# The edge features' product, split into end rows first and source rows later

## The chip, the cores and the metric

The kernel runs on one core of a Trainium2 chip. The metric is the device time of one execution in microseconds (us), lower is better. The times are the median of several runs; the profile is of one further execution, whose times are counted from the start of its span.

## The reference

A graph network and two more layers run on 625 nodes with 512 features. The part that matters here is the attention over 10,000 edges in the second block. Cut to it:

```
h_e = einsum('nf,hfd->hnd', x, W_e)          # 8 heads of 64
h_r = einsum('nf,hfd->hnd', x, W_r)
s_src = einsum('hnd,hd->hn', h_e, a_src)[:, src]
s_dst = einsum('hnd,hd->hn', h_e, a_dst)[:, dst]
diff = h_r[:, dst] - h_r[:, src]
score = s_src + s_dst + einsum('hed,hd->he', diff, a_dif) \
      + einsum('hed,hd->he', abs(diff), a_abs) \
      + einsum('hed,hd->he', h_r[:, src] * h_r[:, dst], a_prd)
alpha = leaky_relu(score, 0.2)
# softmax over the edges of one src, then the sum of att * h_e[dst] into src
```

Beside it stands a linear attention over all nodes (q, k, v from the same normalised x, softmax of k over the nodes, context, output product), whose result is added to x as well.

## The kernel before

The 625 nodes are five tiles of 125 partitions (`NT`), the 512 features four chunks of 128 (`KC`). Each engine has its own block of instructions, and semaphores tie them together. PSUM is a ring of four slots of two banks: `psum_jobs()` lists all uses of it in the order of TensorE's queue, each with the engine (`act` or `dve`) that empties it. `claim` lets TensorE wait until the job that had the slot before has been emptied. Jobs named in `BESIDE_EDGES` share two slots only, since the edge turns hold the other two.

Before the edges, the normalised x is transposed tile by tile (`xnT`, 2). Then TensorE makes `hre`: for each tile a product with `wer`, 1024 columns, the source rows W_e in columns 0 to 511 and the end rows W_r in 512 to 1023. ScalarE copies the W_r half into `hrx` (L1280) and rounds it into `hr_high` (L1283); GpSimd makes the rest `hr_low` (L668). SyncE stores `hrx` to `table` in DRAM. VectorE copies the W_e half into `hea` (L1793), forms per tile three products with the vectors in `ar` (L1799), a difference (L1805) and two reductions (L1802, L1807). The results are the linear terms of the score, one for the node as source and one as destination, in the columns `HD` and `HD + 1` of `hrx`. VectorE then prepares casts and constants and signals `tmp_free` (L1825), since `tmp` lies where the gathers land.

The edges are then taken in 40 turns of 250 edges (`TURNS`), half of them by gathers and half by products:

- GpSimd gathers rows of `table` for both ends (L680), four turns ahead, and scatters the scores into `pairs` (L690), each scatter after the landing of the one before it of the same kind.
- VectorE makes one-hots of the other 125 edges (L1863, L1866). TensorE transposes them (`edge_turn`, L960), ScalarE copies them (L1291), and TensorE multiplies them with `hr_high` and `hr_low` (`edge_product`, L973). VectorE then weighs and reduces both halves (L1872, L1896, L1880).
- Into TensorE's queue, at fixed turns, are put the products of the linear attention: `KEYS`, `QUERIES` (L757), `VALUES` (L748, emptied by VectorE at L1835), `KEYS_TURNED` (L740), `CONTEXT` (L998, emptied at L1846), `ATTENDED`, `PROJECTED` and the transposes `ROWS_TURNED`, which read `hrx` with its linear terms.

TensorE makes the transpose of turn e + 1 before the product of turn e. After the last turn the scattered pairs are loaded and merged (L1930), and a stage over pairs of nodes follows, in which `hea` is multiplied with the weights (L1068).

Of the kernel before, what the change touches and what calls it, by code (L numbers as in the profile page):

```python
# [35 lines left out]
P = 125  # L36
# [54 lines left out]
BESIDE_EDGES = ("kT", "qT", "v1", "kn", "ctx", "oT", "y1", "rT")  # L91

KEYS = (1, 3, 5, 7)
# [11 lines left out]
def psum_jobs():  # L105
# [19 lines left out]
    jobs += [(("hre", i), "dve") for i in range(NT)]  # L125
    for e in range(PROJECTED[-1] + 1):
        for turns, name, who in ((KEYS, "kT", "act"), (QUERIES, "qT", "act"),
# [95 lines left out]
def build_gps(nc, a, out):  # L223
    with ExitStack() as ctx:
# [147 lines left out]
        ar = view(9096, 4, D, parts=P)  # L372
# [3 lines left out]
        tmp = view(18944, 3, D, parts=P)  # L376
# [3 lines left out]
        edge_hots = [view(4220 + N * n, N, parts=P).bitcast(F16)  # L380
# [83 lines left out]
        def _(sp):  # L464
# [68 lines left out]
            for n, name in enumerate(("a_abs", "a_src", "a_dst", "a_dif")):  # L533
                load(ar[:, n, :], row(name), "gat_loaded")
# [4 lines left out]
            for i in range(NT):  # L539
# [3 lines left out]
                load(t[112:P], hrx[112:P, i, :, 0:HD], "table_stored")  # L543
            load(wo1, w("w_outT"), "wo1_loaded")
# [45 lines left out]
        def _(pool):  # L590
# [75 lines left out]
            for i in range(NT):  # L666
                pool.wait_ge(sig("hr_high_ready"), i + 1)
# [28 lines left out]
            pool.wait_ge(sig("tmp_free"), 1)  # L696
# [33 lines left out]
        def _(pe):  # L730
# [217 lines left out]
            for i in range(NT):  # L948
                slot = ring.claim(pe, ("hre", i))
                ring.wait_emptied(pe, ("xnT", 2, i))  # L950
                ring.filled(product(slot, P, nodes(xnT, i), lambda k: wer[:, k, :], KC, 2 * D))
# [13 lines left out]
            def edge_product(e):  # L965
# [10 lines left out]
                last.then_inc(sig("edge_product"), 1)  # L976

# [37 lines left out]
            ring.wait_emptied(pe, ("hre", NT - 1))  # L1015
            pe.wait_ge(sig("hrx_ready"), NT)
            edge_turn(0)
            pe.wait_ge(sig("hr_low_ready"), NT)
            pe.wait_ge(sig("mix1_loaded"), 32)
            for e in range(PROJECTED[-1] + 1):  # L1020
                if e + 1 < TURNS:
                    edge_turn(e + 1)
                if e < TURNS:
                    edge_product(e)
                if e in KEYS:
                    key_or_query("kT", D, KEYS.index(e))
# [10 lines left out]
                if e in ROWS_TURNED:  # L1037
                    h = ROWS_TURNED.index(e)
                    turn(("rT", h), lambda k: hrx[:, k, h, :], [HX] * NT, lambda k: 128 * k)
# [62 lines left out]
        def _(act):  # L1102
# [175 lines left out]
            for i in range(NT):  # L1278
                slot = ring.wait_filled(act, ("hre", i))
                act.activation(hrx[:, i, :, 0:HD],  # L1280
                               slot[0:P, D:2 * D].rearrange("p (h e) -> p h e", h=H), ACT.Copy)\
                   .then_inc(sig("hr_copied"), 1)
                act.activation(hr_high[:, i, :], slot[0:P, D:2 * D], ACT.Copy)\  # L1283
                   .then_inc(sig("hr_high_ready"), 1)
# [794 lines left out]
```

## Time and profile before

| what | us |
|---|---|
| median of 3 runs | 1088.94 |
| lowest and highest | 1088.46, 1090.07 |
| profiled execution, its own time | 1090.06 |
| its span | 1088.2 |
| TensorE matmuls busy (90%) | 982.1 |
| VectorE busy (70%) | 764.0 |
| GpSimd busy (32%) | 347.5 |
| ScalarE busy (31%) | 336.0 |

Shares are of the span. A busy share says how full an engine is on average over stages of different kinds, and not what sets the end. The profile's chain of waits gives TensorE 43%, VectorE 27%, GpSimd 14% and DMA 7% of the span. TensorE's mean granted clock is 0.959 of full speed (2.4 GHz). In a row, the number in square brackets is the idle time of the engine before this instruction and what ended it; an fp32 matmul has two records.

### The profile page before, as it was taken

The numbers are of one execution on the slowest core, as the hardware profiler recorded it, in microseconds if no ns is written. First come the engines' busy times: TensorE is split into PE (matmuls) and PEld (weight loads), VectorE is DVE, ScalarE is ACT, GpSimd is POOL, SyncE is SP. The second block draws the span as 40 slices with busy tenths as digits, with TensorE's granted clock in tenths as the row PEclk, the third lists the DMA queues.
The fourth block names the chain that finished last, engine by engine and source line by source line (L and its number), as shares of the span: only waits on it lengthen the run. The fifth ranks groups of instructions, "written<-read, shape, count | busy, mean of one in ns | idle before, by whom it ended". The sixth has DMA issues, their size and how long they took to land.

```text
span 1088.2 us, 12200 instructions
## 1 busy us (share of the span) xinstructions
PE 982.1 (90%) x4284; PEld 648.8 (60%) x4284; DVE 764.0 (70%) x1320; ACT 336.0 (31%) x613; POOL 347.5 (32%) x316
## 2 busy tenths in 40 slices
PE   7899999999899989999896988999887859988988
PEld 6874686544574447544463436776565528877864
DVE  8897697333795667744435468998987759999743
ACT  5873472312402231122114111321113303444511
POOL 1007720000301102001100116777777714555500
PEclk9999999999999999999898998999988976999999
DMA  9999210203300222001130325333333377541101
GB/s 306 294 306 274 64 79 1 85 12 115 126 1 1 91 59 90 1 0 56 48 115 1 134 48 155 99 99 98 98 93 95 89 284 292 207 163 40 63 1 47
DMA packets 66036, 115.10 MB, mean 106 GB/s; under 512 B 11473, under 2 KB 43473, under 8 KB 64445
## 3 DMA queue, kind: packets, MB, share of 16 engines
q1 hardware_dynamic: 57021, 93.08, 25.3%
q0 software_dynamic: 8960, 21.31, 7.1%
q8 instruction: 32, 0.52, 0.2%
q14 instruction: 23, 0.19, 0.1%
HBM read 85.88 MB, written 28.49 MB: 105 GB/s over the span
## 4 chain that ended last, share of the span: by engine, by line
PE 43%; DVE 27%; POOL 14%; issue 8%; DMA 7%; ACT 1%; SPq 0%; POOLq 0%; DVEq 0%; ACTq 0%
PE ps L748 17%; PE ps L886 7%; POOL arena L680 7%; DMA pairs<-arena,pairi 5%; PE ps L757 5%; DVE arena L1589 5%; POOL pairs L690 4%; PE ps L791 3%; PE ps L740 3%; DVE arena L1945 3%; DVE arena L1930 2%; PE ps L940 2%; DVE arena L1954 2%; PE ps L1093 2%; POOL small L639 1%
## 5 line engine op out<-in xcount | busy, mean ns | idle before, releaser
L748 PE MATMUL ps<-arena 128*125 128x512 f32 x400 | 179.7, 605 | 0.8 <-DVE xn L1623 0.8
L616 POOL TENSOR_TENSOR small<-small 125x1 f32<-125x1 f32 x50 | 34.9, 698 | 390.4 <-DVE small L1402 390.4
L748 PE MATMUL ps<-arena,xnT 128*125 128x512 f32 x280 | 125.7, 607 | 5.0 <-DVE x L1856 4.2
L748 PEld LDWEIGHTS ps<-arena 128*125 128x125 f32 x400 | 75.5, 193 | 90.2 <-issue 89.2
L973 PE MATMUL ps<-ex_low,high 125*125 125x512 f32 x400 | 107.3, 416 | 0.0
L1248 ACT ACTIVATE arena<-ps,cols 128x125 f32<-128x125 f32 x120 | 43.2, 466 | 202.9 <-PE ps L740 202.9
L748 PEld LDWEIGHTS ps<-arena,xnT 128*125 128x125 f32 x280 | 53.5, 193 | 70.4 <-issue 69.0
L690 POOL DMA_INDIRECT pairs<-arena,pairi x80 | 86.9, 1086 | 25.5 <-issue 25.5
L740 PE MATMUL ps<-ident,arena 125*125 125x125 f32 (+3 forms) x425 | 63.0, 285 | 26.5 <-ACT arena L1105 8.8
L973 PEld LDWEIGHTS ps<-ex_low,high 125*125 125x125 f32 x400 | 74.6, 195 | 16.7 <-issue 0.5
L740 PEld LDWEIGHTS ps<-ident,arena 125*125 125x125 f32 (+3 forms) x425 | 54.4, 170 | 48.8 <-issue 17.3
L1105 ACT ACTIVATE arena<-ps 125x625 f32<-125x625 f32 (+4 forms) x79 | 49.3, 648 | 108.1 <-PE ps L740 90.6
L715 POOL TENSOR_TENSOR arena<-arena,counts 125x625 f32<-125x625 f32 x40 | 57.4, 1436 | 78.6 <-ACT arena L1356 35.5
L757 PE MATMUL ps<-arena 66*125 66x313 f32 (+3 forms) x176 | 61.0, 475 | 17.3 <-DVE small L1945 8.6
L886 PE MATMUL ps<-arena 128*125 128x512 f32 x160 | 70.5, 593 | 1.7 <-DVE arena L1594 1.7
L791 PE MATMUL ps<-arena 125*125 125x314 f16 x400 | 57.3, 305 | 6.8 <-DVE arena L1445 5.7
L791 PEld LDWEIGHTS ps<-arena 125*125 125x125 f16 x400 | 54.9, 140 | 9.1 <-DVE arena L1445 7.1
L1356 ACT ACTIVATE arena<-arena,small 125x625 f32<-125x625 f32 x40 | 32.7, 818 | 86.7 <-DVE arena L1954 86.7
L1657 DVE TENSOR_TENSOR x<-x,ps 125x512 f32<-125x512 f32 x30 | 20.5, 685 | 55.1 <-PE ps L748 23.3
L1681 DVE TENSOR_TENSOR arena<-ps,arena 125x512 f32<-125x512 f32 x15 | 10.4, 691 | 65.0 <-PE ps L748 65.0
L1880 DVE TENSOR_REDUCE arena<-arena 125x8 f32<-125x512 f32 x80 | 54.6, 682 | 1.4
L1945 DVE CUSTOM_DVE_ANT_0 arena<-ps,arena 125x625 f32<-125x625 f32 x40 | 51.6, 1290 | 2.3 <-PE ps L757 2.1
(215 smaller groups left out, 1811.6 us busy)
## 6 DMA issues: line engine op xcount, KB each, us to landing
pairs<-fill SPq DMA_DIRECT2D x10, 2500.0 KB, 21.9
arena<-in_mw SPq DMA_DIRECT2D x6, 2048.0 KB, 8.4
arena<-pairs SPq DMA_DIRECT2D x4, 2500.0 KB, 13.9
arena<-pairs SPq DMA_DIRECT2D x8, 1250.0 KB, 6.0
arena<-pairs SPq DMA_DIRECT2D x8, 625.0 KB, 6.4
arena<-in_rows SPq DMA_DIRECT2D x16, 250.0 KB
arena<-in_qkv_w SPq DMA_DIRECT2D x1, 3072.0 KB
arena<-in_cw SPq DMA_DIRECT2D x3, 1024.0 KB, 5.3
```

Source lines behind the costliest of these rows:

```text
L680: pool.indirect_dma_start(out=rows[:, g % GATHERS, :], out_offset=None, in_=table, in_offset=bass.IndirectOffsetOnAxis(ap=ends[:, 2 * g:2 ...
L690: pool.indirect_dma_start(out=pairs[n], out_offset=bass.IndirectOffsetOnAxis(ap=pairi[:, t:t + 1], axis=0), in_=sc[:, t % SCORES, :], in_o ...
L715: pool.tensor_tensor(Sg, Sg, counts[:, i, 0:N].bitcast(F32), ALU.mult).then_inc(sig("pair_weighted"), 1)
L740: last = pe.transpose(slot[0:n, at:at + rows], src, ident[0:rows, 0:rows])
L748: last = mm(slot[0:m, lo:hi], lhsT_of(k), rhs_of(k)[:, lo:hi], start=(k == 0), stop=(k == ks - 1))
L757: last = mm(slot[0:m, at + lo:at + hi], lhsT_of(k), rhs_of(k)[:, lo:hi], start=(k == 0), stop=(k == ks - 1))
L791: last = mm(ps[0:P, 512 * i:512 * i + HALF], one_hot[:, k, 0, P * i:P * (i + 1)], one_hot[:, k, 1, 0:HALF], start=False, stop=False, skip_ ...
L886: last = mm(slot[0:P, lo:lo + 512], nodes(hT, i)(k), w1[:, k, lo:lo + 512], start=(k == 0), stop=(k == KC - 1))
L973: last = mm(product_at[0:P, at:at + D], hotsT[e % 2][:, i, :], part[:, i, :], start=(part is hr_high and i == 0), stop=(part is hr_low and ...
L1589: st.did(v.reciprocal(r, r))
L1880: v.tensor_reduce(sc[0:P, t % SCORES, :], src.rearrange("p (h e) -> p h e", h=H), AX_X, ALU.add)\
L1945: ring.emptied(v.tensor_tensor_reduce(Sg, slot[0:P, across_banks(N)], p3[:, :, h], -1.0, 3e38, ALU.add, ALU.min, smax[:, 0, h:h + 1]), ("p ...
```

## The change

The product `hre` is split. First come the end rows alone, one product of 512 columns per tile (`hr`), emptied by ScalarE. The source rows are a job of their own (`he`, function `sources`), for tile 0 before the first turn's product and for the other tiles in turns 0, 25, 27 and 28 (`HE`). They share the two slots of the linear attention and are emptied by ScalarE, which writes `hea`.

The linear terms are no longer formed from the rows. Since they are linear in the normalised x, the vectors are multiplied into the weights instead: VectorE folds `wer` with `a_dst` (`fold_destinations`, between the normalisations of the tiles) and with `a_src` and `a_dif` minus `a_abs` (`fold_sources`, after the first one-hots) into 16 columns per chunk, `terms`. `sources` multiplies these along with the source rows, and ScalarE copies the 16 results into `hrx`. The vectors are loaded over 128 partitions. `tmp` and its signal `tmp_free` are gone. The edge one-hots move to another place in SBUF; the load of `w_outT` now waits until the last source rows are there, since it overwrites `wer`.

```
-    jobs += [(("hre", i), "dve") for i in range(NT)]
+HE = (-1, 0, 25, 27, 28)
+    jobs += [(("hr", i), "act") for i in range(NT)] + [(("he", 0), "act")]
...
@@ SyncE
+            ring.wait_emptied(sp, ("he", NT - 1))
             load(wo1, w("w_outT"), "wo1_loaded")
...
@@ GpSimd
-            pool.wait_ge(sig("tmp_free"), 1)
             pool.wait_ge(sig("spare_loaded"), 32)
...
@@ TensorE
-                ring.filled(product(slot, P, nodes(xnT, i), lambda k: wer[:, k, :], KC, 2 * D))
+                ring.filled(product(slot, P, nodes(xnT, i), lambda k: wer[:, k, D:2 * D], KC, D))
...
+            def sources(i):
+                slot = ring.claim(pe, ("he", i))
+                for k in range(KC):
+                    mm(slot[0:P, 0:D], xnT[:, k, P * i:P * (i + 1)], wer[:, k, 0:D],
+                       start=(k == 0), stop=(k == KC - 1))
+                    last = mm(slot[0:P, D:D + 2 * H], xnT[:, k, P * i:P * (i + 1)],
+                              terms[:, k].rearrange("p n h -> p (n h)"),
+                              start=(k == 0), stop=(k == KC - 1))
+                ring.filled(last)
...
-            ring.wait_emptied(pe, ("hre", NT - 1))
-            pe.wait_ge(sig("hrx_ready"), NT)
+            ring.wait_emptied(pe, ("hr", NT - 1))
             edge_turn(0)
+            pe.wait_ge(sig("terms_ready"), KC)
+            sources(0)
             pe.wait_ge(sig("hr_low_ready"), NT)
             pe.wait_ge(sig("mix1_loaded"), 32)
             for e in range(PROJECTED[-1] + 1):
                 if e + 1 < TURNS:
                     edge_turn(e + 1)
                 if e < TURNS:
                     edge_product(e)
+                if e in HE:
+                    sources(HE.index(e))
...
@@ ScalarE
+            def sources(i):
+                if i == 0:
+                    act.wait_ge(sig("hea_ready"), 2)
+                slot = ring.wait_filled(act, ("he", i))
+                act.activation(hea4[:, i, :, 0:HD],
+                               slot[0:P, 0:D].rearrange("p (h e) -> p h e", h=H), ACT.Copy)
+                ring.emptied(act.activation(
+                    hrx[:, i, :, HD:HX],
+                    slot[0:P, D:D + 2 * H].rearrange("p (n h) -> p h n", n=2), ACT.Copy), ("he", i))
...
@@ VectorE
+            def fold_destinations(k):
+                st.did(TT(folds[:, 0, :], wer[:, k, 0:D], a_ends[:, 1, :], ALU.mult))
+                st.wait()
+                v.tensor_reduce(terms[:, k, 0, :], by_head(folds[:, 0, :]), AX_X, ALU.add)\
+                    .then_inc(sig("folded"), 1)
+                v.wait_ge(sig("folded"), k + 1)
+            def fold_sources(k):
+                st.did(TT(folds[:, 1, :], wer[:, k, 0:D], a_ends[:, 0, :], ALU.mult))
+                st.did(TT(folds[:, 2, :], wer[:, k, D:2 * D], a_ends[:, 2, :], ALU.mult))
+                st.wait()
+                st.did(TT(folds[:, 1, :], folds[:, 1, :], folds[:, 2, :], ALU.subtract))
+                st.wait()
+                v.tensor_reduce(terms[:, k, 1, :], by_head(folds[:, 1, :]), AX_X, ALU.add)\
+                    .then_inc(sig("terms_ready"), 1)
+                v.wait_ge(sig("terms_ready"), k + 1)
             for i in range(NT):
                 add_to_x(("f0o", i), i)
                 ring.wait_emptied(v, ("f0o", i))
                 stats_of_x(i)
                 if i:
                     normed_x(i - 1)
+                    fold_destinations(i - 1)
             normed_x(NT - 1)
-            for i in range(NT):
-                slot = ring.wait_filled(v, ("hre", i))
-                v.wait_ge(sig("hr_high_ready"), i + 1)
-                ring.emptied(v.tensor_copy(hea4[:, i, :, 0:HD],
...
...
             one_hots_of_edges(0)
             one_hots_of_edges(1)
+            for k in range(KC):
+                fold_sources(k)
```

## Rows read from the trace of the kernel before

**Rows 1.** Chain of waits, from 596 us: start, us, what.
```profile
613.37 34.96 PE ps L748 x80
...
655.93 0.03 DVEq L1825
...
656.94 1.57 POOL arena L680
```
**Rows 2.** Windows of the edge turns: busy us of each engine, clock, DMA.
```profile
700.00:750.00 50.00, 49.36 (x236) 36.66 (x235) 44.62 (x72) 12.70 (x20) 39.03 (x37) 1.00 0.35 97
750.00:800.00 50.00, 44.56 (x198) 30.41 (x197) 45.07 (x74) 9.25 (x14) 38.72 (x38) 0.95 0.36 99
```
**Rows 3.** Timeline, ScalarE's copy of tile 2, TensorE's first turns: start, us, instruction.
```profile
634.62 0.60 ACT L1280 ACTIVATE arena<-ps 125x512 f32<-125x512 f32 x1 [5.78 <-PE ps L748]
...
657.49 0.76 PE L960 MATMUL ps<-arena 125*125 125x125 f16 x5 [9.18 <-DVE arena L1866]
...
659.65 3.75 PE L973 MATMUL ps<-ex_low,high 125*125 125x512 f32 x10
```
**Rows 4.** Window of half a us after tile 2's store; last column GB/s.
```profile
638.50:639.00 0.50, 0.50 (x2) 0.19 (x1) 0.47 (x2) 0.00 (x0) 0.00 (x0) 1.00 0.01 2
```
**Rows 5.** Timeline, VectorE's last two normalisations before the edges.
```profile
610.36 0.54 DVE L1410 TENSOR_SCALAR xn<-x,small 125x512 f32<-125x512 f32 x1
...
611.34 0.88 DVE L1410 TENSOR_SCALAR xn<-x,small 125x512 f32<-125x512 f32 x1 [0.44 <-POOL small L616]
```
**Rows 6.** Narrow matmuls in the chain; VectorE's groups: busy, mean ns.
```profile
189.73 1.72 PE ps L838 x16
...
907.67 2.05 PE ps L1068 x10
...
L1799 DVE TENSOR_TENSOR arena<-arena 125x512 f32<-125x512 f32 x15 | 10.8, 769 | 0.2
...
L1880 DVE TENSOR_REDUCE arena<-arena 125x8 f32<-125x512 f32 x80 | 54.6, 682 | 1.4
```
**Rows 7.** Timeline of GpSimd, scatters of turns 2, 31 and 39.
```profile
678.67 0.99 POOL L690 DMA_INDIRECT pairs<-arena,pairi  x1 [0.31 <-issue]
...
838.64 0.99 POOL L690 DMA_INDIRECT pairs<-arena,pairi  x1 [0.30 <-issue]
...
875.69 0.97 POOL L690 DMA_INDIRECT pairs<-arena,pairi  x1 [0.34 <-issue]
```
**Rows 8.** Timeline of VectorE in the edge turns; last, the merges' group.
```profile
675.61 0.69 DVE L1880 TENSOR_REDUCE arena<-arena 125x8 f32<-125x512 f32 x1
...
783.82 0.69 DVE L1896 TENSOR_TENSOR arena<-arena 125x512 f32<-125x512 f32 x1 [0.94 <-DMA arena<-table,dsti]
...
817.34 0.69 DVE L1896 TENSOR_TENSOR arena<-arena 125x512 f32<-125x512 f32 x1 [0.88 <-DMA arena<-table,dsti]
...
828.58 0.69 DVE L1872 SCALAR_TENSOR_TENSOR arena<-ps,arena 125x512 f32<-125x512 f32 x1 [4.25 <-PE ps L973]
...
870.15 0.69 DVE L1872 SCALAR_TENSOR_TENSOR arena<-ps,arena 125x512 f32<-125x512 f32 x1 [3.48 <-PE ps L973]
...
L1930 DVE TENSOR_TENSOR arena<-arena 125x625 f32<-125x625 f32 x40 | 34.6, 880 | 2.7 <-DMA arena<-pairs 2.7
```
**Rows 9.** Timeline of TensorE in the edge turns.
```profile
706.25 4.37 PE L757 MATMUL ps<-xnT,arena 128*128 128x312 f32 x16
710.47 0.45 PE L960 MATMUL ps<-arena 125*125 125x125 f16 x5
...
715.81 4.37 PE L757 MATMUL ps<-xnT,arena 128*128 128x312 f32 x16
...
787.17 0.78 PE L740 MATMUL ps<-ident,arena 128*125 128x128 f32 x5 [1.97 <-DVE xn L1835]
...
788.97 3.94 PE L973 MATMUL ps<-ex_low,high 125*125 125x512 f32 x10
...
822.99 2.45 PE L757 MATMUL ps<-arena 128*128 128x312 f32 x4 [8.18 <-DVE arena L1846]
```

More of the change, by code:

```diff
@@ L124, in psum_jobs @@
                    lambda i: [], lambda i: [(("xnT", 2, i), "act")])
-    jobs += [(("hre", i), "dve") for i in range(NT)]
+    jobs += [(("hr", i), "act") for i in range(NT)] + [(("he", 0), "act")]
     for e in range(PROJECTED[-1] + 1):
-        for turns, name, who in ((KEYS, "kT", "act"), (QUERIES, "qT", "act"),
+        for turns, name, who in ((HE, "he", "act"), (KEYS, "kT", "act"), (QUERIES, "qT", "act"),
                                  (VALUES, "v1", "dve"), (KEYS_TURNED, "kn", "act"),
@@ L371, in build_gps @@
         wer = view(5000, KC, 2 * D)
-        ar = view(9096, 4, D, parts=P)
+        a_abs = view(9096, D)
+        a_ends = view(24100, 3, D)
+        folds = view(0, 3, D)
+        terms = small[:, 128:192].rearrange("p (k n h) -> p k n h", k=KC, n=2)
         hea = view(11144, NT * H * (HD + 1) + WIDE - HD - 1, parts=P)
@@ L532, in _ @@
             load(wer, w("w_er"), "gat_loaded")
-            for n, name in enumerate(("a_abs", "a_src", "a_dst", "a_dif")):
-                load(ar[:, n, :], row(name), "gat_loaded")
+            load(a_abs, row("a_abs", 128), "gat_loaded")
+            for n, name in enumerate(("a_src", "a_dst", "a_dif")):
+                load(a_ends[:, n, :], row(name, 128), "gat_loaded")
             ring.wait_emptied(sp, ("f0o", NT - 1))
@@ L948, in _ @@
             for i in range(NT):
-                slot = ring.claim(pe, ("hre", i))
+                slot = ring.claim(pe, ("hr", i))
                 ring.wait_emptied(pe, ("xnT", 2, i))
-                ring.filled(product(slot, P, nodes(xnT, i), lambda k: wer[:, k, :], KC, 2 * D))
+                ring.filled(product(slot, P, nodes(xnT, i), lambda k: wer[:, k, D:2 * D], KC, D))
             turned, product_at = ring.psum[2], ring.psum[3]
@@ L1329, in _ @@
                     edge_turned(e)
+                if e - 1 in HE:
+                    sources(HE.index(e - 1))
                 if e - 1 in KEYS:
@@ L1822, in _ @@
             st.did(v.memset(sc, 0.0))
+            flat = hea[:, 0:NT * H * (HD + 1)]
+            v.memset(flat.rearrange("p (g e) -> p g e", e=HD + 1)[:, :, HD:HD + 1], 1.0)\
+                .then_inc(sig("hea_ready"), 1)
+            v.memset(hea[:, NT * H * (HD + 1):], 0.0).then_inc(sig("hea_ready"), 1)
+            st.did(TT(a_ends[:, 2, :], a_ends[:, 2, :], a_abs, ALU.subtract))
+            st.did(TS(a_abs, a_abs, 2.0, None, ALU.mult))
             st.did(TS(minus_ident, ident[0:P, 0:P], -1.0, None, ALU.mult))
             st.wait()
-            v.sem_inc(sig("tmp_free"), 1)
             def k_largest(j):
```

47 lines of the change are left out of this document (12 added, 35 removed).

## The prediction, on record before the result

> **What bounds the kernel now.** I read the chain of waits first, for the stretch from the end of the first expert layer to the edge turns. One piece stands out, TensorE's 80 matmul records of the `hre` products, 34.96 us; then VectorE's work on the last tile; then the queue of VectorE, whose `tmp_free` lets GpSimd begin its gathers at 656.94 [rows 1]. From there the chain runs through GpSimd's gathers and scatters and their landings for all 40 turns. A product of 512 columns costs 0.43 us per record: 34.96 / 80 = 0.437, of which 0.65 us is a start at the lower clock.
>
> Second, who is how far ahead in the edge turns. GpSimd starts the scatter of turn 2 at 678.67, of turn 31 at 838.64 and of turn 39 at 875.69, so (838.64 - 678.67) / 29 = 5.5 us per turn while it also gathers [rows 7]. VectorE has turn 2's score at 675.61 + 0.69 = 676.30, 2.4 us before GpSimd starts on it; turn 31's at 828.58 + 3.2 = 831.8 (from the read of PSUM to the last reduction are five instructions of 0.68 to 0.69 us each, slightly overlapping, 3.2 us), 6.8 us early; turn 39's at 870.15 + 3.2 = 873.35, only 2.3 us early [rows 7, 8]. So GpSimd sets the pace, but at both ends of the loop another engine is close behind. That engine is TensorE: it is busy 49.36 of 50 us around turns 8 to 17 and 44.56 in the next 50 [rows 2]. There, a key or query product takes 710.47 - 706.25 = 4.22 us, and two times `edge_turn` with its product 715.81 - 710.47 = 5.34, 2.67 each [rows 9]. From turn 22 to 30 it has slack: VectorE waits for gathers [rows 8], and TensorE waits 1.97 us before turn 26 and 8.18 us for the context [rows 9]. From turn 31 to 39 it is dense again, so what TensorE is late at turn 31 it is late at turn 39.
>
> **Part by part.** (All times in the profiled execution of before: span 1088.2, run 1090.06 us.)
>
> *First tile data.* `fold_destinations` puts a product and a reduction, 0.69 to 0.77 and 0.69 us [rows 6], into each of four passes of VectorE. Three lie where VectorE waits for `f0o`. The fourth lies between the two normalisations at 610.36 and 611.34, where VectorE had 0.4 us of room [rows 5]: tile 4's comes about 1.0 us later, and TensorE's transpose, on the path, with it. Nothing else queued there.
>
> *End rows.* Five products of 512 columns instead of 1024 remove 40 records of 0.43: -17.2 us. The last product ends at 648.33 + 1.0 - 17.1 = 632.2; a longer stay at the low clock may add up to 1 us, I take 0.2. ScalarE's two copies now release the slots: `hr_copied` at 633.0.
>
> *GpSimd's start.* `tmp_free` is gone; what is late next is `table_stored`. In before, tile 2's copy ends at 634.62 + 0.60 = 635.2 [rows 3] and the traffic of its store has ended by 638.5 [rows 4], some 3.4 us. So the table is stored at 636.4 and, with the 0.98 us from VectorE's signal to the first gather [rows 1], the gathers begin at 637.5: 19.4 us earlier. The loads of w_qkvT come before in the same queue and have ended by then. The load of w_outT now waits for the last `sources` (turn 28) and is wanted at turn 34, some 27 us later: nothing.
>
> *VectorE's preparation.* Removed are five tiles of copy, four products or sums and two reductions. Added are `fold_sources`, four times three products and a reduction, about 2.8 us each, 11.2 in all, behind some 2.6 us of casts and memsets and two pairs of one-hots (2.4 us): from 613.2 to about 629.5. TensorE asks for the terms at 633.9, so 4 us cover it; the first sources would wait for what exceeds that.
>
> The folds run beside GpSimd's subtractions, as L1799 did, which took 0.77 us in the mean [rows 6]; three of those per chunk instead of 0.69 are 1 us in all, within the cover. The Trainium skill (GPSIMD Engine Reference, its table at the top) says that GpSimd's SBUF interface is shared with VectorE and contended by instructions with two SBUF inputs, which these are; the row agrees.
>
> *Sources.* Each is four products of 512 columns (3.44 us) and four of 16. No row has 16 columns. The nearest are 96 wide: 16 records (8 matmuls) in 1.72 us, 0.215 us each, and 10 records in 2.05 us, 0.41 each, both from the chain [rows 6]. From below, 16/512 of a wide one would be 0.03. I take 0.215, the 96-wide matmul at its fastest, which a narrower one should not exceed. So a `sources` is 4.3 us (3.6 to 5.1), five are 21.5: more than was removed. The Trainium skill (TensorE: Matmul & The Clock Gate, LDWEIGHTS) says that loading weights scales with their columns, however few columns are streamed; with 125 columns at its rate, twice per fp32 matmul, its estimate is 0.21 us. By the columns streamed alone a `sources` would be 3.6 us; by that page it is the 4.3 that I take.
>
> *The first turns.* TensorE: `edge_turn(0)` from 633.5 (last slot emptied) to 633.95, sources(0) to 638.3, then turn 1 and product 0 to 641.0, sources(1) to 645.3, product 1 to 647.9, key 0 to 652.1. In before product 0 began at 659.65 and took 3.6 us to the next instruction [rows 3]; with 2.67 and 4.22 key 0 ended at 670.1. So TensorE's path is 18.0 us earlier against 19.4 for GpSimd. That includes two gains: in before TensorE idled 9.18 us and ran the first product at the low clock, 3.75 us [rows 3]. Turn 2's margin falls from 2.4 to 1.0 us, it still holds, and grows from there as before.
>
> *The late sources* (in before's times less 19.4, so that GpSimd's own column is unchanged). TensorE's lag of 1.4 is used up by turn 24, where VectorE waited 0.94 us for its gather [rows 8], and less than that a turn earlier. sources(2) starts when v1's slot is free, 787.2, and ends 791.5; kn(1) and product 26 end at 794.9; kn(2), product 27 at 798.2; sources(3), kn(3), product 28 at 805.8; sources(4) at 810.1, product 29 at 812.8, the context at 817.3, product 30 at 820.0. In before VectorE had turn 30's gather, the last that it waited for, at 817.34 [rows 8]; now it gets there at 820.0 + 0.6 = 820.6, 3.3 us later. So 12.9 us of products cost 3.3: the waits of rows 9, and the gather waits, take the rest. The first may run low: product 26 took 3.94 us after the wait of 1.97 [rows 9], and sources(2) may meet that clock, up to 2.5 us more. I take 0.8: TensorE is 4.1 us late at turn 31, whose margin of 6.8 holds.
>
> *The end of the loop.* 4.1 late at turn 39 against a margin of 2.3, with 0.2 us of hand-over: 2.0 us lost. VectorE's last sums into x are then 2.1 us behind the loads of the pairs; VectorE waits 2.7 us for these loads at the first merges [rows 8], so that is hidden. The pair stage and all behind it don't change.
>
> **Sum.** -19.4 + 2.0 = -17.4; 1090.06 - 17.4 = 1072.7. The profiled run is 1.1 above the median of 1088.94, so 1071.5 us.
>
> **Rivals.** (A) TensorE's path becomes the bound sooner: `sources` is 5.1 us and the low clock meets sources(2). Then the first two cost 1.6 us more, the three late ones 2.4, the low clock 1.7: TensorE is up to 4.1 + 5.7 = 9.8 us late at turn 39, 7.7 lost, a gain of 11.7: 1077. For it speaks the 2.05 us row; against it that the 1.72 us row shows 16 narrow records in a row at half that price.
> (B) The work is only moved: none of the late sources falls into a wait, 12.9 + 1.4 = 14.3 us late at turn 39, 12.2 lost, a gain of 7: 1082. Against it stand the 8.18 us, though these are a wait for VectorE's context, which moves along.
> (C) No change: the first gathers still wait, for a term or store that lands near 656. The folds would have to end some 22 us later, or the stores 19 us: 1089. I see nothing for it.
> (D) Slower: TensorE holds 1.2 GHz over all five `sources`, 8.6 us each (twice 4.3), 21.5 us more. Added to the 4.1, and less what turns 22 to 30 absorb (none is left), it is 25.6 late, less 2.3: 23 lost against 19.4, +4: 1093. It decides from 19.4 + 2.1 = 21.5 us late at turn 39. A fall to the low clock is seen after idle only, and the products fill idle: little for it.
>
> **How the numbers follow.** My forecast 0.64, with its own range 1068.5 to 1074.5 (weight price down to 3.6, first start 1 us earlier or later); A 0.22; B 0.08; C 0.03; D 0.03. The range is 1068.5 to 1078, it leaves out B to D and the tails. A measurement can tell 0.2%, 2.2 us, from no change: faster 0.94, same 0.03, slower 0.03.
>
> **What would show it.** Right: one `hr` block of 17 to 18 us ending near 632; the first gather near 637.5, led by a landing of table and not by VectorE; TensorE's gap before the first edge turn of 1 to 2 us; blocks of sources of 4.3 us; GpSimd's scatter of turn 38 some 19 us earlier, and before the last one a wait for VectorE. Wrong: a gap of TensorE before sources(0) (folds late), a first gather after 640 (stores), matmuls of 16 columns at 0.4 us, or scatters that wait for scores before turn 35.

## The result, and the profile after

The changed kernel takes 1073.25 us in the median of 4 runs (1071.32 to 1078.3), against 1088.7 for the kernel before (4 runs, 1087.45 to 1090.07): a ratio of 0.9865 with a 95% interval of 0.9829 to 0.9901, 1.35% faster. The profiled run took 1073.43 us, its span is 1071.6, and TensorE's mean granted clock 0.967. Against the profiled run of before that is 16.6 us less; the forecast from there was 17.4 less. A second set of 5 runs of the changed kernel (below) gave 1073.97; over both sets the median is 1073.8.

The chain of waits of the changed kernel, between the expert layer and the first gathers (start, us, what), answers to [rows 1]:

```profile
609.20 0.71 DVE stat L1429
...
611.39 0.69 DVE small L1812
...
612.71 1.09 PE ps L744 x4
613.80 19.16 PE ps L752 x40
...
634.23 2.65 DMA table<-arena
637.18 1.30 POOL arena L685
```

The 80 records of 34.96 us have become 40 of 19.16. VectorE's reductions and its signal are gone from the chain; the landing of the table stands in their place. The second line is the new fold of the fourth weight chunk: it lies on the path. 40 records at 0.43 would be 17.2 us; the other 2 us are the clock, as the windows show (after the stretch and its length: busy us of PE, PEld, DVE, ACT and POOL, then clock, DMA share, GB/s):

```profile
608.00:611.00 3.00, 0.99 (x6) 0.55 (x5) 2.42 (x6) 0.59 (x1) 0.62 (x1) 0.97 0.25 35
611.00:614.00 3.00, 2.19 (x9) 1.74 (x9) 2.87 (x14) 0.75 (x2) 0.79 (x2) 0.50 0.98 393
614.00:618.00 4.00, 4.00 (x6) 1.51 (x5) 3.90 (x8) 0.43 (x1) 0.00 (x0) 0.54 1.01 421
618.00:622.00 4.00, 4.00 (x10) 1.69 (x9) 3.90 (x6) 1.09 (x2) 1.52 (x1) 1.00 0.46 144
```

The third number from the right is the granted clock: 0.50 (1.2 GHz) from 611 until near 618, though TensorE is busy without a gap from 614 on.

TensorE at the start of the turns, in its timeline (in brackets the idle time before, and what ended it), and the group rows of the new matmuls:

```profile
634.12 0.50 PE L964 MATMUL ps<-arena 125*125 125x125 f16 x5 [1.18 <-ACT ex_low L1301]
634.46 1.07 PE L985 MATMUL ps<-arena,xnT 128*125 128x512 f32 x2
635.37 0.29 PE L987 MATMUL ps<-small,xnT 128*125 128x16 f32 x2
635.50 1.10 PE L985 MATMUL ps<-arena,xnT 128*125 128x512 f32 x2
...
638.74 0.48 PE L964 MATMUL ps<-arena 125*125 125x125 f16 x5
639.02 2.56 PE L977 MATMUL ps<-ex_low,high 125*125 125x512 f32 x10
```

```profile
L987 PEld LDWEIGHTS ps<-small,xnT 128*125 128x125 f32 x40 | 7.5, 187 | 9.7 <-issue 9.7
...
L987 PE MATMUL ps<-small,xnT 128*125 128x16 f32 x40 | 5.8, 219 | 0.0
```

One `sources` is 638.74 - 634.46 = 4.28 us. From wide matmul to wide matmul it is 1.08 us at most places, so the narrow one adds 1.08 - 0.86 = 0.22 us. No wait for a term stands before it, and the first product takes 2.56 us where before it took 3.75 [rows 3].

Later, VectorE's copy of the values, VectorE's context and GpSimd's scatters (three timelines: TensorE's, the queue of SP, and GpSimd's):

```profile
767.98 1.12 PE L985 MATMUL ps<-arena,xnT 128*125 128x512 f32 x2 [1.05 <-DVE xn L1865]
...
806.88 2.45 PE L761 MATMUL ps<-arena 128*128 128x312 f32 x4 [6.35 <-DVE arena L1876]
...
809.62 3.74 PE L977 MATMUL ps<-ex_low,high 125*125 125x512 f32 x10
```

```profile
791.43 0.39 SPq L469 DMA_DIRECT2D arena<-in_w_outT  x1
```

```profile
796.67 1.48 POOL L695 DMA_INDIRECT pairs<-arena,pairi  x1 [0.76 <-DMA pairs<-arena,pairi]
799.78 0.99 POOL L695 DMA_INDIRECT pairs<-arena,pairi  x1 [1.63 <-DMA pairs<-arena,pairi]
```

The waits of 1.97 and 8.18 us [rows 9] have become 1.05 and 6.35: the late source rows filled part of them. The two scatters wait for the landing of the scatter before, a wait that the kernel before has nowhere near this place. They come just behind the load of w_outT. The window of these 4 us shows the traffic that they meet (columns as above):

```profile
794.00:798.00 4.00, 4.00 (x41) 4.00 (x39) 2.77 (x6) 0.00 (x0) 2.93 (x3) 1.00 1.01 308
```

It has 308 GB/s and all DMA engines full, where the same 4 us of the clock before move 43 GB/s.

The last turn, in the timelines of VectorE and GpSimd, and VectorE's merges:

```profile
855.16 0.69 DVE L1902 SCALAR_TENSOR_TENSOR arena<-ps,arena 125x512 f32<-125x512 f32 x1 [3.57 <-PE ps L977]
...
857.68 0.69 DVE L1910 TENSOR_REDUCE arena<-arena 125x8 f32<-125x512 f32 x1
...
877.92 1.53 DVE L1962 TENSOR_TENSOR arena<-arena 125x625 f32<-125x625 f32 x2 [3.01 <-DMA arena<-pairs]
```

```profile
859.29 0.97 POOL L695 DMA_INDIRECT pairs<-arena,pairi  x1 [0.51 <-issue]
```

Turn 39's score is ready at 857.68 + 0.69 = 858.37 and its scatter starts at 859.29, 0.92 us later; before, 2.34 lay between them [rows 7, 8].

Where the 16.6 us of the two profiles come from: first gather 656.94 to 637.18, -19.76; scatter of turn 39 counted from the first gather, 218.75 to 222.11, +3.36; from there to the pair stage +0.87; from the pair stage to the end of the span 193.18 to 192.11, -1.07. Sum -16.6.

### The profile page after: what moved, and what is told of

Its sections match the earlier page's. It is cut to its first block, busy times and chain, and to the rows that moved or that the text cites. A ratio compares the mean times of both kernels' runs of the same rounds, so it can differ in the third digit from the quotient of the medians.

```text
span 1071.6 us, 12287 instructions
## 1 busy us (share of the span) xinstructions
PE 979.7 (91%) x4324; PEld 648.0 (60%) x4324; DVE 759.3 (71%) x1309; ACT 338.8 (32%) x623; POOL 349.8 (33%) x316
## 4 chain that ended last, share of the span: by engine, by line
PE 40%; DVE 28%; POOL 14%; issue 8%; DMA 7%; ACT 1%; SPq 0%; POOLq 0%; DVEq 0%; ACTq 0%
PE ps L752 16%; PE ps L890 7%; POOL arena L685 6%; DMA pairs<-arena,pairi 5%; DVE arena L1620 5%; POOL pairs L695 4%; DVE arena L1977 4%; PE ps L761 4%; PE ps L795 3%; PE ps L744 3%; DVE arena L1962 2%; DVE arena L1986 2%; PE ps L944 2%; PE ps L1111 2%; POOL small L644 1%
## 5 line engine op out<-in xcount | busy, mean ns | idle before, releaser
L752 PEld LDWEIGHTS ps<-arena 128*125 128x125 f32 x400 | 75.6, 194 | 91.0 <-issue 89.8
L752 PE MATMUL ps<-arena,xnT 128*125 128x512 f32 x240 | 108.7, 610 | 5.0 <-DVE x L1886 4.2
L977 PE MATMUL ps<-ex_low,high 125*125 125x512 f32 x400 | 104.2, 406 | 0.0
L744 PE MATMUL ps<-ident,arena 125*125 125x125 f32 (+3 forms) x425 | 62.4, 283 | 25.9 <-ACT arena L1123 10.0
L752 PEld LDWEIGHTS ps<-arena,xnT 128*125 128x125 f32 x240 | 46.0, 194 | 60.9 <-issue 59.5
L744 PEld LDWEIGHTS ps<-ident,arena 125*125 125x125 f32 (+3 forms) x425 | 53.5, 168 | 47.7 <-issue 19.4
L977 PEld LDWEIGHTS ps<-ex_low,high 125*125 125x125 f32 x400 | 72.1, 188 | 15.9 <-issue 0.5
L761 PE MATMUL ps<-arena 66*125 66x313 f32 (+3 forms) x176 | 59.8, 468 | 16.2 <-DVE small L1977 8.2
L890 PEld LDWEIGHTS ps<-arena 128*125 128x125 f32 x160 | 29.6, 187 | 38.9 <-issue 35.8
```

Of the source, the lines that this page charges most:

```text
L744: last = pe.transpose(slot[0:n, at:at + rows], src, ident[0:rows, 0:rows])
L752: last = mm(slot[0:m, lo:hi], lhsT_of(k), rhs_of(k)[:, lo:hi], start=(k == 0), stop=(k == ks - 1))
L761: last = mm(slot[0:m, at + lo:at + hi], lhsT_of(k), rhs_of(k)[:, lo:hi], start=(k == 0), stop=(k == ks - 1))
L890: last = mm(slot[0:P, lo:lo + 512], nodes(hT, i)(k), w1[:, k, lo:lo + 512], start=(k == 0), stop=(k == KC - 1))
L977: last = mm(product_at[0:P, at:at + D], hotsT[e % 2][:, i, :], part[:, i, :], start=(part is hr_high and i == 0), stop=(part is hr_low and ...
```

## Experiments

All kernels were timed beside the kernel before, in three sets: after_again to both with 5 rounds (before: 1089.08), wout_twice to release_alone with 4 (1089.39), the last four with 4 (1089.56). One kernel's runs lie 2 to 10 us apart, so the stages inside the profiles are compared as well. A profile's span also holds differences that no edit explains: the fourth normalisation, up to which VectorE's program is the same in all kernels of the split, starts between 608.8 and 612.8 us. In the table, "norm to gather" runs from VectorE's fourth normalisation to GpSimd's first gather. The three columns after it are counted from the first gather: GpSimd's scatter of turn 31 (the first of the two scatters of the turn), turn 39's score ready, scatter of turn 39. "Falls" means that the granted clock goes to 0.50 there.

| kernel | median (low to high) | norm to gather | clock at 611 | scatter 31 | score 39 | scatter 39 |
|---|---|---|---|---|---|---|
| before | 1089.1 | 46.6 | falls | 181.7 | 216.4 | 218.8 |
| changed (first profile) | 1073.25 (1071.3 to 1078.3) | 26.96 | falls | 184.5 | 221.2 | 222.1 |
| after_again | 1073.97 (1072.1 to 1078.2) | 27.07 | falls | 183.2 | 221.3 | 221.6 |
| wout_mostly_early | 1069.92 (1068.2 to 1070.4) | 24.54 | stays | 184.0 | 220.8 | 221.7 |
| late_quarter | 1071.90 (1068.5 to 1076.0) | 26.97 | falls | 184.6 | 221.2 | 222.1 |
| both | 1071.42 (1068.2 to 1076.1) | 24.53 | stays | 183.3 | 218.1 | 220.4 |
| wout_twice | 1074.13 (1068.9 to 1074.7) | 24.55 | stays | 185.9 | 224.0 | 224.3 |
| all_first | 1083.62 (1079.4 to 1089.5) | 24.56 | stays | 196.5 | 231.3 | 233.5 |
| one_more_late | 1078.09 (1076.4 to 1080.9) | 27.01 | falls | 183.7 | 225.1 | 225.4 |
| release_alone | 1087.56 (1084.9 to 1093.3) | 41.24 | stays | 185.8 | 220.5 | 222.8 |
| fold_after | 1072.44 (1067.5 to 1073.0) | 25.00 | falls | 183.9 | 220.6 | 221.5 |
| wout_early_again | 1075.18 (1071.1 to 1075.3) | 27.00 | falls | 183.9 | 221.9 | 222.2 |
| best | 1069.90 (1067.6 to 1071.0) | 24.99 | falls | 182.6 | 220.6 | 220.8 |
| best_proj | 1072.10 (1069.7 to 1072.6) | 25.03 | falls | 184.7 | 220.5 | 223.1 |

**1. The changed kernel again** (after_again, no edit).

> The changed kernel once more, beside the others of this call. Each theory expects what its first runs gave: 1071 to 1075 us against about 1088.7 of before, the first gather near 637.2, the last scatter near 860.7 of the span.

The result repeats, ratio 0.9865 (0.9838 to 0.9892). It also gives the scatter between two profiles of one kernel: 1.3 us at the scatter of turn 31, 0.5 at that of turn 39.

**2. The load of w_outT placed early, the late source rows cut, and both.** The first edit:

```
+            for k in range(3):
+                load(wo1[k], w("w_outT")[:, k, :], "wo1_early")
...
-            load(wo1, w("w_outT"), "wo1_loaded")
+            load(wo1[3], w("w_outT")[:, 3, :], "wo1_loaded")
```

> Three of the four chunks of w_outT are loaded before the edge turns into other places, one chunk and b_out stay behind the last sources: 0.5 MB there instead of 1.25. Theory 1: the load beside turns 26 to 28 makes the scatters land late (waits of 0.76 and 1.63 us where 0.3 is usual), so GpSimd's scatter of turn 31 comes 1 to 1.5 us earlier against its first gather; but VectorE has turn 39's score only 0.9 us before GpSimd starts on it, so no more than 0.9 us reach the end: 0.3 to 0.9 us faster than the changed kernel. Rival: GpSimd was slower for another reason (its descriptor work beside more of VectorE's or TensorE's): scatter 31 stays where it is, same time.

The second edit leaves out three of the four chunks of the source rows' products of tiles 2 to 4:

```
-                for k in range(KC):
+                for k in range(KC if i < 2 else 1):
...
```

> The products of source rows for tiles 2 to 4 take one of four chunks only (the results of these tiles are wrong): 3.2 us less TensorE work in each of turns 25, 27 and 28, 9.7 in all. Theory 1: GpSimd's own chain sets the end of the turns by 0.9 us, so TensorE's work there is worth nothing: within 1 us of the changed kernel, though VectorE has turn 39's score some 3 to 5 us before GpSimd wants it. Rival (TensorE's path is the bound at turn 39, as the prediction had it): 2 us faster.

> Both edits: w_outT mostly loaded early, and a quarter of the late sources (results of tiles 2 to 4 wrong). Theory 1: with TensorE out of the way the whole of the load's price comes back, 1.5 to 2.5 us faster than the changed kernel, more than the two edits alone give in sum (0.3 to 0.9 and 0). Rival (one cause alone): the sum of the two.

The medians are 1069.92 (ratio 0.982, 0.9799 to 0.9842), 1071.9 (0.9843, 0.9812 to 0.9873) and 1071.42 (0.9848, 0.9823 to 0.9874): by them the three can hardly be told apart, and the stages must. In its first profile the early load took the waits for landings away between 775 and 830 us: no scatter there waits for one. Yet turn 39's score came at 220.8 after the first gather instead of 221.2. Cutting 9.7 us of TensorE's late work moved it not at all (221.2): there TensorE waits 2.56 us at 784 and 9.21 us for the context instead,

```profile
784.52 0.50 PE L964 MATMUL ps<-arena 125*125 125x125 f16 x5 [2.56 <-DVE arena L1897]
...
793.34 0.50 PE L964 MATMUL ps<-arena 125*125 125x125 f16 x5 [1.49 <-DVE arena L1897]
...
805.44 2.45 PE L761 MATMUL ps<-arena 128*128 128x312 f32 x4 [9.21 <-DVE arena L1877]
```

and one scatter still waits 2.29 us for a landing. (Above is TensorE's timeline in the kernel late_quarter.) Only both edits together bring 3.1 us, 218.1. So two things seem to lie side by side between turns 25 and 31, and whoever takes away one finds the other. That rests on one profile of each kernel; the score of turn 39 differs by only 0.1 us between the two profiles of the changed kernel. The first kernel's median was 4 us under the changed kernel's, which its score column cannot explain; 2.4 of the 4 lie in the stage before the first gather, where its edit does nothing that I can name. That led to experiment 7.

**3. The load made twice** (wout_twice: one more load of w_outT behind the first).

> The load of w_outT behind the last source rows is made twice, so that the traffic that meets the pairs' scatters lasts twice as long. If this load is what makes the scatters land late (theory), GpSimd's scatters near turns 27 to 30 wait 1.5 to 3 us longer for landings than in the changed kernel, and turn 31's scatter starts at 186.5 to 187.5 us after the first gather instead of 183.2 to 184.5; the end of the run moves by at most that, 0 to +2.5 us (1074 to 1076.5). If TensorE's late rows alone set the loop's end (rival), nothing moves by over 0.5 us. The clock of TensorE should fall at about 611 us as in the three kernels whose load stays in one piece behind the last source rows; if it does not, the placement of the load is not what decided that.

Missed in size: turn 31's scatter was expected at 186.5 to 187.5 and came at 185.9. Two scatters wait for landings, 1.34 and 1.65 us; in the changed kernel it is 0.76 and 1.63. From the second scatter of turn 24 to that of turn 31 it takes 41.0 us, as in the changed kernel (40.8 and 39.5 in its two profiles). Over the profiles of the split that stretch is 40.7 us in the mean with the late load (six profiles, 39.5 to 41.4) and 39.5 with three quarters of it early (five, 38.9 to 40.2); before it was 38.8. So the load costs GpSimd some 1.1 us, with ranges that overlap, and a second one adds nothing that shows. The clock at 611 us did not fall here, though the load is late: by the expectation's own test, the placement of the load does not decide that. What made this kernel's score 39 late by 2.8 us stands for the most part in TensorE's timeline: sources(2) came after a wait of 1.95 us instead of 1.05 and ran at the low clock at first, 6.0 us instead of 4.3.

```profile
766.52 1.35 PE L987 MATMUL ps<-arena,xnT 128*125 128x512 f32 x2 [1.95 <-DVE xn L1867]
767.66 0.44 PE L989 MATMUL ps<-small,xnT 128*125 128x16 f32 x2
767.95 2.05 PE L987 MATMUL ps<-arena,xnT 128*125 128x512 f32 x2
```

The Trainium skill (DMA: Bandwidth & Descriptors, SWDGE vs HWDGE vs iDMA) says that inside each DMA engine hardware and software queues feed different internal queues, between which the engine goes round robin. By that rule a scatter beside a load should get its turns, late but not stalled until the load has ended. The trace agrees in part. The changed kernel's traffic fills the DMA engines from 794 to 799. The scatter that starts at 790.85 has landed before 796.67, in the midst of it; the one that starts at 792.34 has landed only at 799.01, 6.67 us later (the median is 2.4), as the traffic ends. The second does not tell taking turns from waiting for the end.

**4. All source rows first** (all_first: the five products between the first transpose and the first product).

```
-HE = (-1, 0, 25, 27, 28)
+HE = ()
...
-            sources(0)
+            for i in range(NT):
+                sources(i)
```

> All five products of source rows stand between the first edge turn's transpose and its product, none later. If the four later ones cost TensorE little because they fall into waits there (theory, a price of about 4 us for 12.9 us of products), all of it now comes before the first product: product 0 starts about 17 us later than in the changed kernel, GpSimd's first score scatter too, and since GpSimd has four turns of gathers to do meanwhile, about 10 us of it show: 1082 to 1085. Rival: the place does not matter, because the same products are made and the loop has only to absorb them: 1074, within 2 us of the changed kernel.

As the theory had it: 1083.62, 9.8 us over the changed kernel's 1073.8. (Its runs lie 10 us apart, 1079.4 to 1089.5. Counted from the first gather, turn 39's scatter is 11.4 us later; in its profile the clock stayed up before the gathers, 2.4 us the other way. Its load of w_outT starts at 654.93, and so meets no late scatter.) The price stands in one line of GpSimd's timeline:

```profile
660.43 1.01 POOL L695 DMA_INDIRECT pairs<-arena,pairi  x1 [15.24 <-DVE arena L1912]
```

GpSimd has made its gathers ahead and waits 15 us for the first score. From the first scatter to turn 39's this kernel takes 208.2 us, as before (208.1); the changed kernel takes 210.8. So spreading takes away 14 us at the front and gives back 2.6 behind: placing products into waits is worth about 11.4 us here.

**5. One more source tile late** (one_more_late: tile 1 in turn 24 instead of turn 0, `HE = (-1, 24, 25, 27, 28)`).

> The source rows of tile 1 move from turn 0 to turn 24, nothing else. Theory (turns 22 to 30 of TensorE have room, the first turns have little): turn 2's scatter is no longer close behind its score, its margin goes from 0.7 to about 5 us; at the loop's end TensorE is 0 to 3 us later since its room is used up, so the time is 0 to +3 us against the changed kernel: 1074 to 1077. Rival (the room is not used up by three late ones): margins at turn 39 as in the changed kernel, 0.3 to 0.9 us, and no change within 1 us.

Even beyond the theory's upper end: 1078.09, 4.3 us more, one whole `sources`. Turn 2's margin went from 0.7 to 4.9 us, as expected, and was of no use. Turn 39's score is 3.9 us later. GpSimd shows it (its timeline, turn 39):

```profile
863.14 1.17 POOL L695 DMA_INDIRECT pairs<-arena,pairi  x1 [4.56 <-DVE arena L1910]
```

TensorE's timeline shows what the fourth late tile does, here and then in the changed kernel:

```profile
768.10 1.10 PE L744 MATMUL ps<-ident,arena 128*125 128x128 f32 x5 [2.29 <-DVE xn L1865]
...
772.96 1.02 PE L985 MATMUL ps<-arena,xnT 128*125 128x512 f32 x2
```

```profile
763.55 0.71 PE L744 MATMUL ps<-ident,arena 128*125 128x128 f32 x5
...
767.98 1.12 PE L985 MATMUL ps<-arena,xnT 128*125 128x512 f32 x2 [1.05 <-DVE xn L1865]
```

The source rows and the linear attention share two slots, so one more job in front shifts which job has to wait for VectorE's last copy of the values (L1865). In the changed kernel it is sources(2); here it is the turned keys (L744) one place earlier, and an edge turn with its product comes behind the wait too. These take 4.86 us from 768.10 to 772.96, against 3.2 for the same three at full speed, since the clock is low (0.53 of full speed from 769 to 772). Counted from the first gather, sources(2) starts 4.4 us later, of which 1.65 is the clock. So the fourth tile costs about its full length, by the shared slots and the clock; that the room itself is used up is not shown.

**6. The release alone** (release_alone: the kernel before, scratch moved away from the gathers' landing place, GpSimd's wait for it gone, products as before).

```
-        tmp = view(18944, 3, D, parts=P)
+        tmp = view(24100, 3, D, parts=P)
...
-            pool.wait_ge(sig("tmp_free"), 1)
...
-            v.sem_inc(sig("tmp_free"), 1)
```

> The kernel before with the two places of scratch moved apart, so that GpSimd's first gather no longer waits for VectorE's signal; products, linear terms and all else stay. The gather then waits for the last store of the table: about 3.6 us earlier, 653.3 instead of 656.9. Theory (before, GpSimd's column is 2.4 us behind TensorE's at turn 2 and at turn 39, so TensorE takes over when GpSimd starts earlier): 2.1 us of the 3.6 arrive, 1087.0 against 1089.1. Rival (GpSimd's start alone decides): all 3.6 arrive, 1085.5. Rival (the release was no part of the gain): 0.

Counted from the fourth normalisation, the first gather is 5.3 us earlier. From the end of the products it takes 650.57 - 646.24 = 4.3 us, against 656.94 - 648.33 = 8.6 before: 4.3 us are the release (I had put 3.6), and the other 1.0 goes with TensorE's clock, which stayed up. Then it is given back; the chain of waits of this kernel shows to whom:

```profile
611.89 34.35 PE ps L747 x80
...
657.93 3.92 PE ps L972 x10
...
665.37 1.01 POOL pairs L690
```

TensorE's products, through VectorE's term work, release the first scatter (it waits 4.16 us for the score), which comes 1.2 us earlier than before, counted from the same normalisation. The median is 1.8 us lower, ratio 0.9994 (0.9975 to 1.0013): no difference that these runs can tell. The 2.1 us of the theory and none at all both fit, the rival's 3.6 does not. In the kernel before, GpSimd's chain was only a few us longer than TensorE's; the release without the shorter products brings next to nothing. The other half, the split with the signal kept, was not run.

**7. The fold behind the last normalisation, and the load again.**

```
                 if i:
                     normed_x(i - 1)
+                if 0 < i < NT - 1:
                     fold_destinations(i - 1)
             normed_x(NT - 1)
+            fold_destinations(KC - 1)
```

> The changed kernel with the fold of the last chunk for the destinations put behind VectorE's last normalisation instead of before it. Theory (that fold delays the fifth tile's normalisation and with it the end rows' product by about 1 us, as predicted): the last normalisation starts about 0.8 us after the fourth one instead of 2.3, TensorE's last transpose and the product of the end rows about 0.9 to 1.3 us earlier, the first gather too; the run 0.9 us less, 1073.1 against 1074.0. Rival (the gap is set by GpSimd's statistics or by the slot that ScalarE empties, not by the fold): no change. Whether TensorE's clock falls at 611 us is a separate matter of about 2.4 us either way; it fell in four and did not fall in four of the eight profiles of kernels with the split so far.

> The kernel with three of the four chunks of w_outT loaded before the turns, a second time, on another run of the chip. If its 1069.9 was due to the placement of the load (theory A), it comes out at 1069 to 1071 again, 3 to 4 us under the changed kernel. If it was the clock at 611 us, which did not fall in that profile and did in the changed kernel's, and which the load cannot reach (theory B), the profile may show either, and the median lies between 1070 and 1074: the profile with a fall has its first gather 2.4 us later than the one without.

The gap between the last two normalisations went back from 1.89 to 0.98 us, as in before. From the fourth one to the first gather the kernel with the edit takes 25.0 us, with the clock falling, where the changed kernel takes 27.0 with the clock falling: 2.0 us for one product and one reduction of 1.4 us in sum. Against the profiles in which the clock stays (24.55, below) it is no gain, and no profile with the edit shows the clock staying. TensorE and the windows of the kernel best, which has the same edit, show how (columns as above; to be read against those of the changed kernel):

```profile
610.49 1.10 PE L746 MATMUL ps<-ident,xn 125*128 125x125 f32 x4 [2.01 <-DVE xn L1444]
611.82 1.09 PE L746 MATMUL ps<-ident,xn 125*128 125x125 f32 x4 [0.23 <-DVE xn L1444]
```

```profile
611.00:614.00 3.00, 2.77 (x9) 1.75 (x8) 2.87 (x8) 1.18 (x2) 0.48 (x1) 0.51 1.00 406
614.00:618.00 4.00, 4.00 (x10) 1.68 (x9) 3.89 (x14) 1.05 (x2) 0.00 (x0) 1.00 1.02 425
```

The fall itself is the same, but TensorE's second wait is 0.23 us instead of 0.81, and the clock is back at 614 instead of near 618. Of the 2.0 us, 0.6 is the later data (the normalised tile is there 1.86 instead of 2.44 us after the fourth normalisation began), the rest the shorter stay.

The repeated early load came out at 1075.18, not at 1069 to 1071, and its profile shows the fall and 27.0 us. So theory A is out. Theory B's sign is there, though the median is 1.2 us over its range. The same stretch in the first profile and then in the second (each time a line of TensorE's timeline and a window):

```profile
610.45 0.65 PE L746 MATMUL ps<-ident,xn 125*128 125x125 f32 x4 [2.01 <-DVE xn L1444]
...
614.00:618.00 4.00, 4.00 (x11) 1.70 (x10) 3.89 (x9) 1.08 (x2) 0.36 (x1) 1.00 1.02 424
```

```profile
612.87 1.08 PE L746 MATMUL ps<-ident,xn 125*128 125x125 f32 x4 [2.01 <-DVE xn L1444]
...
614.00:618.00 4.00, 3.23 (x7) 1.89 (x8) 3.83 (x17) 1.17 (x2) 0.00 (x0) 0.50 1.01 422
```

The two spans differ by 5.4 us: 2.5 in this stage, 2.4 before the fourth normalisation, where the programs are the same, and 0.4 up to the scatter of turn 39. The early load by itself shows no gain there: 221.7 and 222.2 us after the first gather, against 222.1 and 221.6 in the changed kernel. Over the nine profiles with the fold in its old place, the stage takes 27.0 us where the clock falls (five profiles, 26.96 to 27.07) and 24.55 where it stays (four, 24.53 to 24.56), behind the same wait of 2.01 us. The Trainium skill (TensorE: Matmul & The Clock Gate, Part 1) says that the point at which the clock goes up differs from run to run of one kernel; here it is the fall that came in one profile of a kernel and not in the other.

**8. Both edits, and one projection moved behind the turns** (best; best_proj, with `PROJECTED = (34, 36, 40, 41, 42)`).

> Both edits together: three of the four chunks of w_outT loaded before the turns, and the last fold for the destinations behind the last normalisation. If both are additive: 0.9 us under the kernel with the early load alone, 1069 to 1071. If the load is worth nothing by itself (the two causes at the loop's end overlap): as the kernel with the later fold alone.

> Both edits together and, besides, the projections of the last three node tiles put behind the edge turns (turn numbers 34, 36, then 40, 41, 42 instead of 34, 36, 38, 40, 41), so that one product of 4 us leaves the dense turns 31 to 39. Theory (TensorE is what ends the loop): turn 39's score is ready 3.5 to 4 us earlier relative to the first gather, its margin of 0.9 us grows to 2.3 or more, the last scatter comes 1.4 to 2 us earlier. What follows the loop then holds the projection that was moved, 4.2 us of TensorE behind VectorE's last turn; the pair stage begins with waits for the pairs' loads and merges of 35 us on VectorE, in which it is hidden: in sum 1 to 2 us less than both edits together. Rival: the sums into x behind it delay VectorE's merges, and the gain is given back: no change.

Both edits give 1069.9 (1067.6 to 1071.01), ratio 0.9811 (0.9788 to 0.9833), against the changed kernel's 0.9865 (0.9829 to 0.9901, and 0.9838 to 0.9892 in the second set): the lowest median here, about 4 us under the changed kernel, though not timed in one set with it. Against fold_after alone (0.9795 to 0.9848) it cannot be told apart; from the fourth normalisation to the scatter of turn 39 it takes 245.8 us against 246.5. Moving a projection did what it should on TensorE: from turn 31's read of PSUM to turn 39's it takes 38.3 us instead of 41.7, and the last margin is 2.6 instead of 0.3 us. But GpSimd needs 38.3 to 38.4 us from scatter 31 to scatter 39 in both, and in this profile it was 2.1 us later at turn 31. TensorE was later there too, by 3.35 us, with a fall of the clock at sources(2) that best does not have, so turn 39's score comes no earlier (220.5 against 220.6). The time is 1072.1, no gain; GpSimd's own column, the chain of its gathers and scatters, sets the last scatter in this profile.

## Why the prediction was right, and where its sizes were off

The forecast was 1071.5 us with a range of 1068.5 to 1078; measured were 1073.25 and 1073.97. The likeliest case came about, and its mechanism for the most part: two chains shortened together, and a price for the late source rows at the loop's end. In part the sum is lucky, since errors cancel in it. By its steps:

- **End rows.** Removed 17.2 us, as put: 40 records. Their end was forecast for 632.2; ScalarE's last copy starts at 632.98. The step that was mis-sized is "a longer stay at the low clock may add up to 1 us, I take 0.2". Measured: 2.45 us between a fall and none (nine profiles); against before, whose clock fell too but came back just after 614, it is 19.16 - 17.2 less 0.65, 1.3 us.
- **The fourth fold.** Forecast 1.0 us. The data is 0.6 us later, but with the clock it costs 2.0 (fold_after). Fold and clock were costed apart; they are one effect, since the fold lengthens TensorE's second wait.
- **The first gather.** Forecast 637.5, measured 637.18, led by the table's landing. It is right because two errors cancel: the table is stored at 636.88 instead of 636.4, but from there to the gather it is 0.3 us and not the 0.98 that rows 1 show from VectorE's signal.
- **Folds hidden.** The last ended at 631.0 instead of 629.5: of eight products three met a subtraction of GpSimd and took 1.35 to 1.67 us instead of 0.68, mean 1.0 and not 0.77. The cover of 4 us became 3.4 (TensorE reached the terms at 634.4): it held.
- **Sources.** 4.3 us forecast, 4.28 measured; 0.22 us for a narrow matmul, taken as 0.215. Rival A needed 5.1.
- **Turn 2.** Margin 1.0 forecast, 0.71 measured.
- **The late sources.** TensorE late by 3.3 us plus 0.8 of clock was forecast, in all 4.1. Measured at turn 31's read, counted from the first gather: 171.64 to 176.29, 4.65. The first product that reads the context (L761) starts 3.65 us later, and the remaining 1.0 is product 31, 3.74 us at the low clock against 2.73. The fall that I had placed at sources(2) did not come in this profile. It came near there in three others, behind waits of 1.94 to 2.29 us (wout_twice, one_more_late, best_proj: 0.53 to 0.74 of full speed from 769 to 772). The fall behind the context, which before has too, lasted longer.
- **The load of w_outT, "nothing".** This step failed. It was costed by when its data are wanted, not by what its traffic meets: GpSimd's scatters wait 2.4 us in sum for landings, and GpSimd's column loses about 1.1 us up to turn 31. At the end of the loop moving the load by itself brought nothing that shows.
- **The loop's end.** Forecast 2.0 us lost at the scatter of turn 39, measured 3.4 and 2.8 in the two profiles. Turn 39's score is 216.4 to 221.2, 4.8 us, late; less the margin of 2.3 and with 0.3 of hand-over that is 2.7. In the first profile GpSimd's own column is 0.6 later still. So two of the signs did not come: turn 38's scatter was to be some 19 us earlier and is 16.4 (872.84 to 856.45), and the last turn's scatter was to wait for VectorE. In the first profile it waits for nothing (0.51 "issue"), in the second 1.21 us for a landing. The forecast had TensorE and VectorE alone behind the 2.0 us; GpSimd's own column is late as well.
- **Behind the loop, "unchanged".** From the last scatter to the pair stage 17.8 before, 18.8 and 18.5 now, and VectorE's merges wait 3.4 us for the pairs instead of 2.7; from there to the end 193.2, now 192.1 and 192.8. Near enough to nothing in sum.

Of the rivals, A fell with the price of a narrow matmul. B's time, 1082, is near what all_first measured (1083.6), a kernel in which none of the rows is put into a wait. C needed first gathers near 656. For D, no profile shows the low clock over a whole `sources`. The median missed the forecast by 2 us, no more than the runs of one kernel lie apart; the load, the clock and the fold are terms of about 1 us each that were put too low.

What stays open: what decides, behind one and the same wait, whether the clock falls at 611 us; where the 4 us between profiles before the fourth normalisation come from; and why two equal profiles of GpSimd's column differ by 1.3 us at turn 31.

## What to carry to other kernels

When two engines' chains run side by side at nearly equal length, ask for each edit by how much it shortens both: the release alone brought 5.3 us at the first gather and nothing that could be told at the end, and two causes of delay at turns 25 to 31 seem to hide each other until both are removed. Put extra products into an engine's waits, and count how many fit: three blocks of 4.3 us cost 3.7 us together, the fourth cost 4, by a slot that it shared and the low clock behind a longer wait. Before a wait of TensorE is lengthened even by half a us, look at the clock behind it; and cost a moved load by the transfers that it meets as well as by its due time.

## What the runs showed of the hardware

- Behind a wait of 2.01 us, the same in nine profiles, TensorE's granted clock fell to 0.50 in five and stayed at 1.00 in four; a fall cost the stage up to the first gather 2.45 us. With 0.6 us less of waiting behind it (0.23 instead of 0.81) the clock came back some 3.5 us earlier.
- An fp32 matmul of 128 x 125 weights by 16 columns adds 0.22 us to a stream of wide ones. Its two weight loads take 187 ns each, 0.37 together, so a part of them runs beside other matmuls.
- VectorE's product of two SBUF operands, 128x512 fp32, took 0.68 us alone and 1.35 to 1.67 us in the three cases that met a subtraction of GpSimd (here the one of 1.52 us from 620.42). The one reduction that met one, at 630.36, stayed at 0.69, as the others did:

```profile
620.21 0.69 DVE L1818 TENSOR_TENSOR arena<-arena 128x512 f32<-128x512 f32 x1
620.82 1.67 DVE L1819 TENSOR_TENSOR arena<-arena 128x512 f32<-128x512 f32 x1
...
623.25 0.69 DVE L1823 TENSOR_REDUCE small<-arena 128x8 f32<-128x512 f32 x1
```

(VectorE's timeline in the changed kernel.)
